# A deformable-convolution pipeline on one core: every slot's three weighted tiles are summed before one fold, the second and third weighted in PSUM

## What is computed

```
x = x + L0(_gn(x))   # Winograd convolution, 6x6 tiles
x = x + L1(_gn(x))   # deformable convolution, 3x3 taps, 8 groups
x = x + L2(_gn(x))   # four quantised 3x3 convolutions and one 1x1
x = x + L3(_gn(x))   # 3x3 convolution plus edge term, channel attention
```

```
for yi, xi, wgt in corners:          # four corners of each point
    valid = (yi >= 0) & (yi < H) & (xi >= 0) & (xi < W)
    out = out + x[:, clip(yi), clip(xi)] * (wgt * valid)
y = einsum('bgikhw,goik->bgohw', sampled, dconv_w) + dconv_b
```

## Time and profile before

| | |
|---|---|
| Median of 3 runs | 4324.02 us (4323.59 to 4336.19) |
| Profiled execution, span from first to last instruction | 4328.9 us |
| TensorE busy, matmuls | 4115.4 us, 95% |
| VectorE busy | 3191.3 us, 74% |
| ScalarE busy | 1827.2 us, 42% |
| GpSimd busy | 3159.8 us, 73% |
| DMA | 1022.57 MB, mean 236 GB/s |

### The profile page before, as it was taken

How to read it: one execution, slowest core, us unless ns; L and a number is a source line. 1 busy time by engine, 2 the same in 40 slices (tenths; PEclk the granted TensorE clock), 3 DMA queues, 4 the chain that set the end, 5 groups by cost and what they waited for, 6 DMA issues and landing times.

```text
span 4328.9 us, 61705 instructions
## 1 busy us (share of the span) xinstructions
PE 4115.4 (95%) x21925; PEld 1924.0 (44%) x21925; DVE 3191.3 (74%) x6460; ACT 1827.2 (42%) x2008; POOL 3159.8 (73%) x3094
## 2 busy tenths in 40 slices
PE   2899999999999999999999999999999999999993
PEld 2444444444444444444444444444444444444441
DVE  4757787777877777787777877877787777877663
ACT  1344444444444434444444444444444444444431
POOL 1777777777777777777777777777777777777750
PEclk8899999999999999999999999999999999999996
DMA  4677787878878788887877878787887878878762
GB/s 111 216 234 245 238 263 220 265 227 248 256 235 263 227 250 258 245 256 229 261 233 246 270 233 261 223 251 249 245 258 232 258 234 253 260 237 258 240 194 64
DMA packets 480231, 1022.57 MB, mean 236 GB/s; under 512 B 262164, under 2 KB 298356, under 8 KB 475636
## 3 DMA queue, kind: packets, MB, share of 16 engines
q1 hardware_dynamic: 283252, 460.40, 34.7%
q10 hardware_dynamic: 98400, 356.97, 25.4%
q0 software_dynamic: 98304, 201.52, 16.5%
HBM read 862.19 MB, written 73.20 MB: 216 GB/s over the span
## 4 chain that ended last, share of the span: by engine, by line
PE 72%; DVE 13%; POOL 5%; issue 4%; DMA 3%; SPq 1%; ACTq 1%; ACT 1%; POOLq 0%; DVEq 0%
PE ps_r L1506 52%; PE ps_c L1492 5%; POOL ring L599 5%; PE ps_y L1521 4%; PE ps_a L1445 3%; DVE col_hat L1198 2%; PE ps_c L1535 2%; PE ps_a L1492 2%; DMA taps_c<-plane_act 1%; PE ps_y L1542 1%; DVE ps_w L1219 1%; DVE ring L1225 1%; PE ps_a L1483 1%; DVE ring L1221 1%; ACTq L793 1%
## 5 line engine op out<-in xcount | busy, mean ns | idle before, releaser
L599 POOL DMA_INDIRECT ring<-patch_table,idx_part x3072 | 3151.6, 1026 | 1031.6 <-issue 1019.6
L1506 PE MATMUL ps_r<-select,image 128*128 128x512 f32 x6912 | 3160.9, 602 | 21.1 <-DVE col_hat L1198 15.3
L1506 PEld LDWEIGHTS ps_r<-select,image 128*128 128x128 f32 x6912 | 1253.6, 190 | 1424.3 <-issue 1368.9
L1198 DVE TENSOR_TENSOR col_hat<-ps_r,col_hat 128x512 f32<-128x512 f32 x1152 | 790.6, 686 | 919.1 <-PE ps_r L1506 917.8
L649 ACT ACTIVATE select<-row_in,minus_row 128x1536 f32<-128x1536 f32 x384 | 604.8, 1575 | 1042.7 <-PE ps_r L1506 556.9
L651 ACT ACTIVATE select<-select,one_col 128x1536 f32<-128x1536 f32 x384 | 605.3, 1576 | 12.5
L668 ACT COPY samples<-ps_c 128x512 f32<-128x512 f32 x256 | 148.9, 582 | 655.8 <-PE ps_c L1535 655.8
L1219 DVE TENSOR_TENSOR ps_w<-ring,ps_w 128x384 f32<-128x384 f32 x512 | 284.8, 556 | 19.8 <-DMA ring<-patch_table,idx_part 15.2
L1225 DVE TENSOR_TENSOR ring<-ring,ps_w 128x384 f32<-128x384 f32 x512 | 280.3, 547 | 4.4
L1221 DVE TENSOR_TENSOR ring<-ring,ps_w 128x384 f32<-128x384 f32 x512 | 280.2, 547 | 0.0
L1521 PEld LDWEIGHTS ps_y<-col_hat,w_dense 128*32 128x32 f32 x6144 | 143.5, 109 | 297.5 <-issue 245.9
(11 more groups left out here) (233 smaller groups left out, 2588.9 us busy)
## 6 DMA issues: line engine op xcount, KB each, us to landing
col_hat<-coord_table SPq DMA_DIRECT2D x384, 768.0 KB
row_in<-coord_table ACTq DMA_DIRECT2D x384, 768.0 KB
ring<-patch_table,idx_part POOLq DMA_INDIRECT x3072
taps_c<-plane_act SPq DMA_DIRECT2D x135, 268.1 KB
coord_table<-wino ACTq DMA_DIRECT2D x64, 216.0 KB
taps_c<-xn_c ACTq DMA_DIRECT2D x96, 130.0 KB
taps_c<-xn_c SPq DMA_DIRECT2D x96, 130.0 KB
plane_act<-act_c SPq DMA_DIRECT2D x180, 65.0 KB
```

The lines of the kernel that those rows point to most:

```text
L599: nc.gpsimd.indirect_dma_start(out=ring[j][:, h % 2, k, :], out_offset=None, in_=table, in_offset=bass.IndirectOffsetOnAxis(ap=idx_part[:, ...
L1198: v.tensor_tensor(hat_t, ps_r[:, (s + t) % 2], hat_t, ALU.mult).then_inc(tile_weighed, 1)
L1506: ins = mm(ps_r[:, (s + t) % 2], image[:, m, t], select[s % 2][:, m], start=(m == 0), stop=(m == PAIRS - 1))
```

## The change

`SUMMED` becomes all 24 slots, so that every slot has one fold. The sums are made differently: tile 0 is weighted into `col_hat` as before; tiles 1 and 2 are weighted in place in `ps_r`, and added from there to tile 0's product by a second instruction, which waits for the first. `tile_weighed` of tiles 1 and 2 now comes with the addition, so that a half of `ps_r` is freed by it. `sum_tiles` and the semaphore `tiles_summed` are gone, and the fold waits for the slot's last `tile_weighed`. Stages A and C are as they were.

```diff
--- before.py
+++ after.py
@@ -40,7 +40,7 @@
 SLOTS = PARTS * DT
 DSEL = DT * Q
 
-SUMMED = (4, 5, 6, 7, 8, 11, 14, 19, 20, 21, 22, 23)
+SUMMED = range(SLOTS)
 
 ITEMS = DT * PARTS
 
@@ -304,7 +304,6 @@
         select_made = sem("select_made")
         rows_made = sem("rows_made")
         tile_weighed = sem("tile_weighed")
-        tiles_summed = sem("tiles_summed")
         dense_folded = sem("dense_folded")
         turned = sem("turned")
         copied = sem("copied")
@@ -1194,20 +1193,15 @@
                 if t == 0:
                     dve.wait_ge(col_hat_in[s % 3], (n * (SLOTS // 3) + s // 3 + 1) * 16)
                 dve.wait_ge(rows_made, tile + 1)
-                hat_t = col_hat[s % 3][:, t]
-                v.tensor_tensor(hat_t, ps_r[:, (s + t) % 2], hat_t, ALU.mult).then_inc(tile_weighed, 1)
-
-            def sum_tiles(n, s, t):
-
-                hats = col_hat[s % 3]
-                dve.wait_ge(tile_weighed, (n * SLOTS + s) * WT + t + 1)
-                if t == 1:
-                    tiles_added[0] = chain.add(v.tensor_tensor(hats[:, 0], hats[:, 0], hats[:, 1], ALU.add))
+                hat_t, rows_t = col_hat[s % 3][:, t], ps_r[:, (s + t) % 2]
+                if t > 0 and s in SUMMED:
+                    chain.step(v.tensor_tensor(rows_t, rows_t, hat_t, ALU.mult))
+                    total = col_hat[s % 3][:, 0]
+                    dve.wait_ge(tile_weighed, tile)
+                    ins = v.tensor_tensor(total, total, rows_t, ALU.add)
                 else:
-                    chain.upto(tiles_added[0])
-                    v.tensor_tensor(hats[:, 0], hats[:, 0], hats[:, 2], ALU.add).then_inc(tiles_summed, 1)
-
-            tiles_added = [0]
+                    ins = v.tensor_tensor(hat_t, rows_t, hat_t, ALU.mult)
+                ins.then_inc(tile_weighed, 1)
 
             def gathered_tile(g, j):
                 return ring[j][:, g % 2]
@@ -1379,8 +1373,6 @@
                 for q in range(WT):
                     if live(n):
                         weigh_tile(n, s, q)
-                    if q > 0 and s in SUMMED and live(n):
-                        sum_tiles(n, s, q)
                     gathered_block(n, s, q)
                     if (s, q) == (1, 2) and live(n):
                         if not known_zero(n):
@@ -1513,10 +1505,7 @@
                 if e == 0 and (not known_zero(n) or g > 0):
                     pe.wait_ge(conv_saved, n * PARTS + g)
                 for t in range(1 if s in SUMMED else WT):
-                    if s in SUMMED:
-                        pe.wait_ge(tiles_summed, n * len(SUMMED) + SUMMED.index(s) + 1)
-                    else:
-                        pe.wait_ge(tile_weighed, (n * SLOTS + s) * WT + t + 1)
+                    pe.wait_ge(tile_weighed, (n * SLOTS + s) * WT + (WT if s in SUMMED else t + 1))
                     for j in range(JB):
                         ins = mm(ps_y[j * C:(j + 1) * C, :],
                                  w_dense[:, DT - 1 - e].rearrange("p g o -> p (g o)"),
```

## The result

The changed kernel takes 4397.9 us (median of 4 runs, 4395.74 to 4400.11), the kernel before in the same comparison 4328.15 us. The ratio is 1.016, with a 95% interval of 1.0146 to 1.0175: slower, by 70 us. The forecast was 4396.

The account below looks back on a forecast made before the run. TensorE was taken to set the pace, with VectorE full in places. 2.2 + 1.7 + 0.6 + 1.1 = +5.6 us for images 1 to 14, less 3 us each for first and last: +72, 4396 us; range 4350 to 4425.

Parts of the forecast that it names:

- The bound: Whole program: TensorE sets the pace, but VectorE, busy three quarters of the time, has no room in some stretches.
- The folds: TensorE, twelve slots per image: each fold loses two thirds, 5.2 us per image, 83 us in all, the gain's ceiling.
- four places: Slots 0 to 4, 9 and 10, 12 and 13, 15 to 18: added VectorE work delays TensorE, +5.6 us per image.
- The pair: VectorE, tiles 1 and 2: multiplication and dependent addition start 0.72 us apart; 24 additions cost 17.3 us per image.
- The first: Slots 0 to 4: eight additions delay the multiplication of (4,0), so row tile (4,2) waits; +2.2 us per image.
- the walk: Image 8, step by step: additions push VectorE's later work by 0.72 us each where idle time is lacking, until TensorE waits.
- The third: Slots 12 and 13: row tile (13,2) starts 0.7 us late, row tile (14,0) 1.0 us late; +0.6 us per image.
- I give each a gain of 3 us: First image lacks stage C on VectorE, last lacks stage A: each gains 3 us of its 5.2.
- (a): Rival: VectorE's idle quarter hides all additions and the fold savings remain, 4241 us; 4%. Half hidden: 4315 to 4337, 7%.
- (b): Rival: GpSimd's gathers set the pace and get faster without the SBUF-only additions, 4265 to 4310 us; 3%.
- (c): Rival: late results reach the DMA copies for stage C's convolutions, 1 to 2 us more per image, 4410 to 4424; 16%.
- (d): Rival: the change does not do what it says, such as a much slower PSUM multiplication; past 4450 us; 2%.

Follow-up runs that it names:

- the four kernels without one place: Changed kernel with slots 0 to 3, 9 and 10, 12 and 13, or 15 to 18 folded tile by tile again; ratios gave back 11, 21, nothing, 2 us.
- the two faster ones: New form, old twelve slots plus 3, 13, 16: 4308.7 us; kernel before plus 3, 13, 16, 18, slot 18's first addition later: 4316.2 us.
- three kernels with fewer additions and the same wait: Changed kernel with slots 0 to 3, 12 and 13, or 15 to 18 folded tile by tile again; by the ratios 11, nothing and 2 us came back.

## Why the prediction was right

**The bound.** TensorE set the pace, and VectorE's full stretches, not its average load (78% after), set what the additions cost. This was the core, and the four kernels without one place gave the prices back place by place.

**The folds.** 12 x 0.43 us per image was forecast; the folds' busy time fell by 85 us (83 forecast). Little of it reached the time, for the reason given: at four places TensorE waits for a time that VectorE sets.

**The pair.** 0.72 us was taken; 0.71 to 0.73 measured. The multiplication that writes PSUM takes 696 ns (686 into SBUF), the addition 688. The Trainium skill's 65 ns more for a source in PSUM ("VectorE: DVE Perf Modes", the section on the TRN2 errata) did not appear: the additions with both sources in SBUF take 692 and 693 ns in the kernel before.

**The places.** Forecast 2.2, 1.7, 0.6 and 1.1; measured 1.9, 1.65, 0.8 and 1.0. The first was over by 0.3: in image 8 the `var` result came 0.2 us sooner than in the walk and the multiplication of (4,0) 0.4 us sooner, so the idle times took up more than the 0.4 us allowed. The third was under by 0.2: row tile (14,0) came 1.2 us later and not 1.0, and fold 13 gave back 0.36 us and not 0.43.

**What was mis-sized, and where luck helped.** The four places come to 5.4 us per image and not 5.6, 3 us less over fourteen images. The last row of the table takes off another 3 us in twelve images, and that is the event in image 3 of the kernel before: chance, and no term of the sum. "I give each a gain of 3 us" for the first and the last image looks too small, since the two profiled executions differ by 4.3 and 4.6 us there. But these are not the folds. The changed kernel's form with the old set, which saves no fold, has the same two images as the changed kernel: 243.7 and 341.9 us against 243.7 and 341.8, from the first row tile of the image to the next image or the end. The execution of the kernel before lost the time: 3.6 us from (12,2) to (14,1) of the first image, where a row tile waited 3.5 us and not 1.9 and the granted clock was then 0.50 for 3.4 us, and 3.2 us from (11,1) to (12,2) of the last, with a wait of 1.5 us for copies and the same clock. So no run shows the gain of 3 us in either image.

The span grew by 65 us and the median by 70, because of which executions were profiled: a run's time lies 2.0 us above its span, so that the profiled one of the kernel before was some 3 us above its median and that of the changed kernel 2 us below its own. That 4396 met 4397.9 to within 2 us is luck; the mechanism and the size, some 5 us per image at four places, are not.

**The rivals.** (a) fell with 139 us of waits. (b) was no rival, as the gathers were not waited for; their busy time fell by 21 us, about the size that was given. (c), late results reaching the copies, did not come: TensorE's waits for copies fell, from 5.3 us to 1.0 for `plane_act` and from 2.4 to nothing for `xn_c`. Other kernels waited more for them, 9 us in the two faster ones and 14 and 16 us in the two with the mean matmul moved alone. (d) nothing: the multiplication in PSUM takes 696 ns.

**What was not seen.** The text left the clock at 1.00. In the changed kernel this held, once in 13 images apart, but only just: three kernels with fewer additions and the same wait lost 1.7 us in 8 to 10 of 13 images. Had it gone as in those, the changed kernel would have taken some 20 us more, and still have been in the range.

## What to carry to other kernels

The price of an instruction on an engine that is busy three quarters of the time is nothing in one place and its full length in the next; find for each place the next result that another engine waits for, and the idle time between. Then put the instruction only where that idle time covers it: here three of twelve slots, 0.6% faster, against all twelve, 1.6% slower. When taking parts out gives back less than they cost, look at stretches that were not touched before doubting the price, and look at the single images before reading a mean: one late copy moved a mean of twelve by 0.3 us.

## What the runs showed of the hardware

**TensorE's clock after a wait of 1.8 us.** Idle for 1.79 us, TensorE got 1.2 GHz for 3.4 us in 10 of 13 images in one kernel, and in another, with the same wait, in 1 of 13. In the six kernels with a wait of 1.1 us there, the one before among them, it was none of 13. In images 2 to 14 of all fourteen traces TensorE was idle for 0.9 to 1.6 us 378 times, and no stretch of lower clock began behind one of these; each stretch of lower clock there stood behind or in an idle time of 1.7 us or more. In the last image of the kernel before it fell behind one of 1.5 us. What decides among waits of the same length was not settled; no run here varied it on purpose.

**Gathers and VectorE's additions.** The mean gather took 1026 ns before, and varied from kernel to kernel. The page's row of the kernel with all slots in the old form, both operands in SBUF:

```profile
L599 POOL DMA_INDIRECT ring<-patch_table,idx_part x3072 | 3183.7, 1036 | 1077.6 <-issue 1014.0
```
The kernel with 15 slots in the new form:

```profile
L598 POOL DMA_INDIRECT ring<-patch_table,idx_part x3072 | 3088.4, 1005 | 1079.8 <-issue 1010.7
```
The kernel with 16 slots in the old form (its line 600):

```profile
L600 POOL DMA_INDIRECT ring<-patch_table,idx_part x3072 | 3130.8, 1019 | 1045.6 <-issue 1015.6
```
Additions with two operands in SBUF and the mean gather: 1036 ns with 768 of them, 1019 with 512, 1026 and 1027 with 384 (two kernels), 1005 to 1022 with none (ten kernels). The Trainium skill ("GPSIMD Engine Reference", the key points) has GpSimd contend with VectorE's instructions of two SBUF inputs. The most and the fewest such additions agree with that, the 1019 ns with 512 does not, and ten kernels with none differ by 17 ns among themselves, so these runs do not show a size for it. VectorE waited for gathers as little as before (15.4 us at line 1213, 15.2 at 1219) and TensorE for none, so it changed no time that the rows show. Where the 4 us come from by which the old set in the new form ran below the kernel before (ratio 0.9987) was not tested.
